# Latent attention's first weights made behind the experts' last units, and one more sequence of the feed-forward in the drain

## What is computed

```python
x = x + _L0_xattn_ref(_layernorm(x, axis=-1), ctx_512, ctx_512)
x = x + _L0_ffn_ref(_layernorm(x, axis=-1), ...)       # top 2 of 8 experts and 4 pass-through routes
x = x + _L1_xattn_ref(_layernorm(x, axis=-1), ctx_512, ...)
x = x + _L1_ffn_ref(_layernorm(x, axis=-1), ...)       # MX-quantised gate, up, down
```

```python
q_hk = (hidden_q @ Wq.T).reshape(Bv, Sv, H, K)
q_big = jnp.einsum('bshk,hkq->bshq', q_hk, w_kc_q)
q_big = _apply_rope(q_big, sin_q[None, :, None, :], cos_q[None, :, None, :])
kv_r = _apply_rope(kv_c, sin_k[None], cos_k[None])
q_r = jnp.einsum('bshq,hqr->bhsr', q_big, W_qr)
k_r = jnp.einsum('bld,hdr->bhlr', kv_r, W_kr)
attn = jax.nn.softmax(jnp.einsum('bhsr,bhlr->bhsl', q_r, k_r), axis=-1)
ctx_c = jnp.einsum('bhsl,bld->bhsd', attn, kv_r)
ctx_lat = jnp.einsum('bhsd,hkd->bhsk', ctx_c, w_kc_kv)
return ctx_lat.transpose(0, 2, 1, 3).reshape(Bv, Sv, H * K) @ Wo.T
```

## Time and profile before

| | |
|---|---|
| median of 3 runs | 785.99 us |
| lowest, highest | 784.54, 786.02 us |
| the profiled execution | 785.92 us |
| its span, first to last instruction | 783.9 us |
| PE, DVE, ACT, POOL busy | 94%, 75%, 52%, 72% of the span |
| mean granted clock of PE | 0.991 of full speed |

### The profile page before, as it was taken

The page is one execution under the profiler, slowest core; times in us unless marked ns, Lnnn a source line. Parts: engine busy times, 40 slices in busy tenths (PEclk is TensorE's granted clock), DMA queues, the critical chain, the costliest instruction groups (busy, mean ns, idle before and its releaser), DMA issues.

```text
span 783.9 us, 15005 instructions
## 1 busy us (share of the span) xinstructions
PE 733.1 (94%) x4872; PEld 534.6 (68%) x4872; DVE 589.0 (75%) x1077; ACT 405.2 (52%) x1084; POOL 564.7 (72%) x588
## 2 busy tenths in 40 slices
PE   3999999978999999798999999999999999987896
PEld 2655555446888888766787777777777777755554
DVE  5898888948777778776565677676767676768996
ACT  1678878732333233326454454655455544573664
POOL 5667777525777767665757778888788888766895
PEclk9999999979999999999999999999999999999999
DMA  9300000013000001132110000000000000000101
GB/s 252 136 1 0 0 0 1 2 52 127 21 21 21 20 22 59 37 125 102 51 52 1 1 2 1 2 1 1 1 1 2 2 1 2 1 1 2 35 28 48
DMA packets 8764, 24.14 MB, mean 31 GB/s; under 512 B 1711, under 2 KB 5167, under 8 KB 8087
## 3 DMA queue, kind: packets, MB, share of 16 engines
q1 hardware_dynamic: 8154, 23.28, 9.0%
q10 hardware_dynamic: 549, 0.08, 0.1%
HBM read 21.26 MB, written 2.10 MB: 30 GB/s over the span
## 4 chain that ended last, share of the span: by engine, by line
PE 44%; DVE 6%; issue 3%; ACT 3%; POOL 2%; DVEq 0%; POOLq 0%; ACTq 0%
PE ps L1413 17%; PE ps L1462 5%; PE ps L1483 4%; PE ps L1429 4%; PE ps L1447 4%; PE ps L1432 3%; PE ps L1497 3%; PE ps L1324 2%; DVE ps L2172 1%; DVE f_h L2160 1%; ACT p L1573 1%; POOL f_h L2280 1%; ACT f_gated L2124 1%; PE ps L2046 1%; ACT l_y L1563 0%
## 5 line engine op out<-in xcount | busy, mean ns | idle before, releaser
L1758 POOL TENSOR_TENSOR q<-turned 64x512 f32<-64x512 f32 x127 | 166.2, 1309 | 24.2 <-DVE turned L1677 11.4
L1413 PE MATMUL ps<-l_yt,a 128*128 128x512 f32 x576 | 144.1, 400 | 4.0 <-DVE a L1631 2.3
L1413 PEld LDWEIGHTS ps<-l_yt,a 128*128 128x128 f32 x576 | 105.1, 189 | 28.9 <-DVE a L1631 2.9
L1745 POOL TENSOR_TENSOR p<-p,l_inverse 128x512 f32<-128x512 f32 x64 | 66.4, 1040 | 60.1 <-DVE l_inverse L1699 59.2
L1677 DVE TENSOR_TENSOR turned<-ps,rope 128x1024 f32<-128x1024 f32 x64 | 78.0, 1219 | 40.6 <-PE ps L1413 36.3
L881 PE MATMUL ps<-yt_experts,wsplit 128*128 (+1 forms) x384 | 97.3, 403 | 0.1
L468 DVE TENSOR_REDUCE negmax<-ps 128x4 f32<-128x512 f32 x128 | 85.1, 685 | 14.9 <-PE ps L291 13.8
L1573 ACT ACTIVATE p<-ps,l_negmax 128x128 f32<-128x128 f32 x256 | 89.8, 388 | 6.5 <-DVE l_negmax L1668 6.5
L881 PEld LDWEIGHTS ps<-yt_experts,wsplit 128*128 128x128 f32 x384 | 71.6, 193 | 14.5 <-DVE inner L1036 0.3
L384 ACT ACTIVATE pt<-ps 128x512 f32<-128x512 f32 x128 | 69.8, 599 | 5.5 <-PE ps L313 3.7
L1590 ACT ACTIVATE qs<-ps 128x512 f32<-128x512 f32 x32 | 19.1, 597 | 102.6 <-PE ps L1432 102.6
(11 more groups left out here) (231 smaller groups left out, 1563.0 us busy)
## 6 DMA issues: line engine op xcount, KB each, us to landing
wide<-in_wide SPq DMA_DIRECT2D x8, 768.0 KB, 4.3
mx_raw<-in_mx SPq DMA_DIRECT2D x8, 384.0 KB, 3.1
x<-in_x SPq DMA_DIRECT2D x4, 512.0 KB, 8.9
ctx_t<-in_ctx_t SPq DMA_DIRECT2D x1, 2048.0 KB, 7.8
out<-x SPq DMA_DIRECT2D x16, 128.0 KB, 1.7
narrow<-in_narrow SPq DMA_DIRECT2D x8, 192.0 KB, 4.1
ktraw<-in_ctx_rows SPq DMA_DIRECT2D x1, 1248.0 KB
wraw<-in_gate SPq DMA_DIRECT2D x1, 1024.0 KB, 18.7
```

The costliest lines, as they stand in the source:

```text
L1413: out = pe.matmul(tile_bank(n, k), a[i][:, pa, kin, k * 128:(k + 1) * 128], yt[j % 2][:, py, kin, :, :].rearrange("p b s -> p (b s)"), sta ...
L1745: pool.tensor_tensor(p[:, head, :, :], p[:, head, :, :], spread(inverse[:, head, :], 2, S), ALU.mult).then_inc(normed[head], 1)
L1758: t = pool.tensor_tensor(out[rows[(head + half) % 2], head, :], turned[rows[head], half, :], turned[rows[head], 2 + half, :], ALU.add)
```

## The change

It has two parts. The first moves pair 0's weights and group 0's turned rows out of latent's beginning into the experts' functions `last`. Their buffers (a new class `Beginning`) take the place of buffers that are dead by then. On the way the first group's normalisation goes from DVE to ACT, with a shift that POOL computes; DVE's block powers come behind the last inner and h; the last `divide` on POOL comes behind a copy of h; and the first narrow load is issued when the last up products are made. The second part raises `EARLY` to 4 and puts the products, the silu and an inverse scale of sequence 3 by hand into the drain.

The core of the diff:

```diff
@@ routed_experts
+        experts.close()
+        g = Beginning(nc, m, latent)
+        halves_ps, rows_ps = [gate_ps[1], up_ps[1]], [weight_ps, last_weight_ps]
+        context_ps, narrow_ps = gate_ps[1], up_ps[1]
@@ sync
             load_wide(sp, m, d, 0)
+            sp.wait_ge(up_made, UNITS)
+            load_narrow(sp, m, d, 0)
@@ tensor, last
                 down(UNITS - 3)
+                pe.wait_ge(m.wide_loaded[0], 16)
+                pe.wait_ge(gated_made, UNITS)
+                queries_products(pe, m.wide[0], 0, halves_ps[0]).then_inc(g.a_made, 1)
+                pe.wait_ge(inner_made, UNITS)
+                queries_products(pe, m.wide[0], 1, halves_ps[1]).then_inc(g.a_made, 1)
                 turn_tiles(CHUNKS - 2)
                 down(UNITS - 2)
+                for k in range(2):
+                    pe.wait_ge(g.y_made, 2 * k + 2)
+                    pe.wait_ge(h_made, UNITS - 1 + k)
+                    turn_pair(pe, m, g.y, k, rows_ps[k]).then_inc(g.y_turned, 1)
                 down(UNITS - 1)
+                pe.wait_ge(g.a_lo, 1)
+                context_products(pe, m.wide[0], context_ps).then_inc(g.c_made, 1)
+                pe.wait_ge(g.a_lo, 2)
+                pe.wait_ge(m.narrow_loaded[0], 16)
+                narrow_products(pe, m.narrow[0], narrow_ps).then_inc(g.b_made, 1)
                 pe.wait_ge(mx_kept, CHUNKS - 1)
                 turn_tiles(CHUNKS - 1)
@@ scalar, last
                 keep_hidden(UNITS - 1)
+                act.wait_ge(var_made, 4)
+                act.wait_ge(rotated, ROTARY_STEPS * GROUPS)
+                for n in range(4):
+                    act.activation(g.y[:, n, :], m.x[:, n, :], ACT.Identity, bias=g.shift[:, n, :],
+                                   scale=m.rstd[:, n, :]).then_inc(g.y_made, 1)
+                for half in range(2):
+                    act.wait_ge(g.a_made, half + 1)
+                    act.activation(g.a0[:, 0, half, :], halves_ps[half][:, 0:3 * 128], ACT.Copy).then_inc(g.a_hi, 1)
                 keep_tiles(CHUNKS - 2)
+                for k in range(2):
+                    act.wait_ge(g.y_turned, k + 1)
+                    act.activation(g.rows(k, 0), pair_of(rows_ps[k]), ACT.Copy).then_inc(g.y_hi, 1)
+                act.wait_ge(g.c_made, 1)
+                act.activation(g.wc[:, 0, 0, :], context_ps[:, 0:E], ACT.Copy).then_inc(g.c_hi, 1)
+                act.wait_ge(g.b_made, 1)
+                act.activation(g.b[0][:, :, :].rearrange("p k c -> p (k c)"), narrow_ps[:, 0:2 * 128],
+                               ACT.Copy).then_inc(g.b_kept, 1)
                 keep_tiles(CHUNKS - 1)
@@ vector, last
-                block_powers(UNITS, GROUPS - 1, EXPERTS - 2)
...
                 hidden(UNITS + 1, 1, last_weight_ps)
+                block_powers(UNITS, GROUPS - 1, EXPERTS - 2)
+                for half in range(2):
+                    dve.wait_ge(g.a_hi, half + 1)
+                    dve.tensor_tensor(g.a0[:, 1, half, :], halves_ps[half][:, 0:3 * 128], g.a0[:, 0, half, :].bitcast(F32),
+                                      ALU.subtract).then_inc(g.a_lo, 1)
                 shift(UNITS + 1, GROUPS - 1, EXPERTS - 1)
+                for k in range(2):
+                    dve.wait_ge(g.y_hi, k + 1)
+                    dve.tensor_tensor(g.rows(k, 1), pair_of(rows_ps[k]), g.rows(k, 0).bitcast(F32),
+                                      ALU.subtract).then_inc(g.y_lo, 1)
                 dve.wait_ge(down_made, UNITS)
                 add_to_x(GROUPS)
@@ gpsimd, last
                 low_part(UNITS - 3, 1)
+                pool.wait_ge(var_made, 2)
+                pool.wait_ge(up_made, UNITS)
+                pool.tensor_tensor(g.shift[:, 0:4, 0], m.mv[:, 0:4, 0], m.rstd[:, 0:4, 0], ALU.mult).then_inc(var_made, 1)
+                pool.wait_ge(var_made, 3)
+                pool.tensor_scalar(g.shift[:, 0:4, 0], g.shift[:, 0:4, 0], -1.0, None, ALU.mult).then_inc(var_made, 1)
+                low_part(UNITS - 2, 0)
                 divide(CHUNKS - 1, EXPERTS - 2)
-                low_part(UNITS - 2, 0)
                 low_part(UNITS - 1, 1)
@@ latent_attention, sync
-        load_narrow(sp, m, d, 0)
@@ latent_attention, tensor
-        queries_weights(0, 0, m.bank(0))
-        queries_weights(0, 1, m.bank(1))
-        turn(0, 0, w_ps)
-        turn(0, 1, q_ps)
-        context_weights(0, m.bank(2))
-        narrow_weights(0, m.bank(3))
@@ latent_attention, vector
-        normalise_first()
-        split_queries_weights(0, 0, m.bank(0))
-        split_queries_weights(0, 1, m.bank(1))
-        split_rows(0, 0, w_ps)
-        split_rows(0, 1, q_ps)
         split_context_weights(0, m.bank(2))
@@ feed_forward
-    EARLY = 3
+    EARLY = 4
@@ feed_forward, tensor
         products(2, 1)
+        products(3, 0)
         turn_p(END, 0)
...
         context(END)
+        products(3, 1)
         project(END, 0)
@@ feed_forward, scalar
-            if n >= 3 and inside(n - 1, B):
+            if n >= EARLY and inside(n - 1, B):
...
         keep_context(END)
+        silu(3)
+        invert_scale(2, 2)
```

More of the change, by code:

```diff
@@ L1233, in rotate_context, with __init__, rows @@
     step.then_inc(rotated, 1)
+class Beginning:
+    def __init__(self, nc, m, scope):
+        sb = lambda name, shape, dt=F32: scope.enter_context(nc.sbuf_tensor(name, shape, dt))
+        sem = lambda name: scope.enter_context(nc.semaphore(f"l_{name}"))
+        self.y = sb("l_y", [S, 4, E])
+        self.yt1 = sb("l_yt1", [128, 2, HALVES, 4, S], F32R)
+        self.wc = sb("wc", [128, 2, HEADS // 2, E], F32R)
+        self.q0, self.qs = sb("q0", [128, 3, 4 * S]), sb("qs", [2 * CE, 4 * S])
+        self.yt0 = sb("l_yt0", [128, 2, HALVES, 4, S], F32R)
+        self.a0 = sb("a0", [128, 2, HALVES, 3 * 128], F32R)
+        self.b = [sb(f"b{i}", [128, 2, 2 * CE]) for i in range(2)]
+        m.narrow = [sb("narrow0", [2 * CE, 3 * 128])]
+        self.shift = sb("l_shift", [S, B, 1])
+        (self.a_made, self.a_hi, self.a_lo, self.b_made, self.b_kept, self.c_made, self.c_hi, self.c_lo, self.y_made,
+         self.y_turned, self.y_hi, self.y_lo) = (
+            sem(n) for n in ("a_made", "a_hi", "a_lo", "b_made", "b_kept", "c_made", "c_hi", "c_lo", "y_made", "y_turned",
+                             "y_hi", "y_lo"))
+    def rows(self, k, part):
+        return self.yt0[:, part, :, 2 * k:2 * k + 2, :]
@@ new lines, in pair_of, with queries_products @@
+def pair_of(ps):
+    return ps.rearrange("p (h b s) -> p h b s", h=HALVES, b=2)
+def queries_products(pe, wide, half, ps):
+    for head in range(2):
+        wq = wide[:, head, half * 128:(half + 1) * 128]
+        most = ps[:, 0:256].rearrange("p (t h c) -> p t h c", t=2, h=2)[:, :, head, :]
+        rest = ps[:, 256:384].rearrange("p (t h c) -> p t h c", t=2, h=2)[:, :, head, :]
+        for out, columns in ((most, wide[:, head, E:E + 128]), (rest, wide[:, head, E + 128:E + CQ])):
+            t = pe.matmul(out, wq, columns.rearrange("p (t c) -> p t c", t=2), start=True, stop=True)
+    return t
@@ new lines, in context_products, with narrow_products, turn_pair @@
+def context_products(pe, wide, ps):
+    for head in range(2):
+        t = pe.matmul(ps[head * CE:(head + 1) * CE, 0:E], wide[:, head, E + CQ:E + CQ + CE],
+                      wide[:, head, E + CQ + CE:], start=True, stop=True)
+    return t
+def narrow_products(pe, narrow, ps):
+    for k in range(2):
+        t = pe.matmul(ps[:, k * 2 * CE:(k + 1) * 2 * CE], narrow[:, k * 128:(k + 1) * 128],
+                      narrow[:, 2 * 128:], start=True, stop=True)
+    return t
+def turn_pair(pe, m, y, k, ps):
+    out = pair_of(ps)
+    for half in range(HALVES):
+        for s in range(2):
+            t = pe.transpose(out[:, half, s, :], y[:, 2 * k + s, half * 128:(half + 1) * 128], m.ident[:, :])
+    return t
@@ L1259, in latent_attention @@
     m.wide.append(sb("wide1", [KDIM, 2, E + CQ + CE + E]))
-    m.narrow = [sb(f"narrow{i}", [2 * CE, 3 * 128]) for i in range(2)]
-    b = [sb(f"b{i}", [128, 2, 2 * CE]) for i in range(PAIRS)]
-    wc = sb("wc", [128, 2, PAIRS, E], F32R)
-    y, shift = sb("l_y", [S, 4, E]), sb("l_shift", [S, B, 1])
-    yt = [sb(f"l_yt{i}", [128, 2, HALVES, 4, S], F32R) for i in range(2)]
+    m.narrow.append(sb("narrow1", [2 * CE, 3 * 128]))
+    b = g.b + [sb(f"b{i}", [128, 2, 2 * CE]) for i in range(2, PAIRS)]
+    wc, y, shift, yt, qs = g.wc, g.y, g.shift, [g.yt0, g.yt1], g.qs
     turned = sb("turned", [128, 2 * TILES, N])
-    q = [sb(f"q{i}", [128, TILES, N]) for i in range(2)]
-    qs = sb("qs", [2 * CE, N])
+    q = [g.q0, sb("q1", [128, TILES, N])]
     negmax, total, inverse = (sb(f"l_{n}", [S, 2, 4]) for n in ("negmax", "total", "inverse"))
@@ L1272, in latent_attention @@
     with ExitStack() as pairs:
-        a = [pairs.enter_context(nc.sbuf_tensor(f"a{i}", [128, 2, HALVES, TILES * 128], F32R)) for i in range(PAIRS)]
+        a = [g.a0] + [pairs.enter_context(nc.sbuf_tensor(f"a{i}", [128, 2, HALVES, TILES * 128], F32R))
```

(1 more changed line is left out.)

62 lines of the change are left out of this document (15 added, 47 removed).

## The result

| | us, median (lowest to highest) | runs |
|---|---|---|
| before | 786.0 (784.5 to 787.6) | 6 |
| the change | 781.6 (780.2 to 783.7) | 6 |
| ratio | 0.9942, 95% interval 0.9922 to 0.9963 | |

A forecast was written before the change was run, and what follows sets the result against it. TensorE was taken to bound the kernel, busy 733.1 of 783.9 us. Front +0.6, clock there +0.1 and drain -3.2 made -2.5, from 785.9 to 783.4 us; range 782.6 to 785.6.

The forecast's parts named there:

- The front, +0.6: End of experts and latent's preparation: pair 1's products wait for their wide load, starting at 338.0 instead of 337.41.
- DVE's new chain: Front: DVE waits for ACT's first copy of a; its sum into x ends at 333.35 instead of 329.68.
- first tile: Front: the first tile starts with the new block at 333.7, 0.8 us earlier than 334.52.
- The missing DMA wait: Sign: PE waits 1.0 to 1.6 us before pair 1's products; if missing, front term wrong and kernel a microsecond faster.
- rival D: Front: PE's clock falls; 3.5 us of it mostly covered by the load wait, 10 us gives 787.0; chance 0.08.
- my +0.1: Front: cost allowed for a short low-clock stretch, mostly covered by PE's 1.3 us wait for the load.
- The drain, -3.2: Drain: fourth sequence's early products and silu let DVE, POOL and the end come 3.2 us earlier (2.1 + 1.1).
- The gated product: Drain: DVE's fourth gated product comes at 712.75 instead of 714.87, 2.1 us earlier.
- The second part, 1.1 from the chain of ACT and POOL: Drain, 720 to 772.6: DVE's idle of 0.4 for ACT and 0.7 for POOL goes, 1.1 us gained.
- another time than before: Sign: the prediction is wrong if the latent steps between front and drain change their time; no term for them.
- Rival B: Drain gains 2.1 only: PE's clock falls again and ACT's chain stays bound to PE; 784.5 us, chance 0.17.
- C: Front: pair 1's wide load shares engines with the narrow and pair 2's loads, 2.4 us later; 785.8, chance 0.10.

The follow-up runs named there:

- again: The changed kernel run once more, unaltered; 782.48 us, ratio to before 0.9958.
- y_later: The changed kernel with ACT's copies of the pair's two halves kept ahead of the four normalisations of y; 780.32 us, ratio to before 0.9926.
- y_wide_bound: The changed kernel with ACT's two halves ahead of y's normalisations, pair 1's wide load early, second sequence's clip bound read from PSUM; 778.74 us, ratio to before 0.9899.
- before_again: The kernel before, unaltered, for another profile; 786.97 us in one run.
- front_alone: The changed kernel with the drain as it was before, so the front's part only; 785.90 us, ratio to before 1.0006.
- drain_new_places: The kernel before with the drain's part, and latent's first tensors at the change's addresses, instruction order kept; 780.95 us, ratio to before 0.9942.
- drain_alone: The kernel before with the drain's part of the change only; 782.31 us, ratio to before 0.9956.

## Why the prediction was wrong

Two of its steps failed. It priced the latent steps between front and drain at nothing, and they took 0.75 us less. And it worked out the drain's gain as 3.2 us from one execution of the old drain: the stages give 2.9 against that execution and 4.1 against another, the medians 3.6. By its own steps:

- **The front, +0.6 (forecast), +0.5 to +0.6 (change, again): right in size, half wrong in mechanism.** DVE's new chain, the block's end and the first tile (1.0 earlier, 0.8 forecast) came as worked out. The missing DMA wait, which I had named as the sign that this term is wrong, did not make the kernel faster: rival D's mild case came true, half clock for 3.1 us, and it covered the load almost exactly. I had priced that overlap as my +0.1 and thought the clock unlikely to matter; y_later shows the wait of 1.28 us that the half clock hid.
- **The drain, -3.2 (forecast), -2.9 by the profile.** The gated product comes 1.6 us earlier and not 2.1, counted from the last query products. The clip that collided with POOL is the difference: it runs 0.5 us longer than before (1.94 and 1.40), and y_wide_bound gave 0.77 back. The second part, 1.1 from the chain of ACT and POOL, came in full: POOL's run starts 2.7 us earlier, 1.6 and 1.1.
- **The same step against the typical execution: -3.6, not -3.2.** Here lies part of the miss. I took the old drain from one profiled execution, with one half-clock stretch. Two other executions of the old order, of before_again and front_alone, show two, and 1.2 us more. I noted that the clock fell after PE's wait of 2.8 us, and did not ask what the wait of 2.25 at 711.2 would do in another execution.
- **Latent's steps, "another time than before" as a sign of error: it was one.** -0.75 us, priced at nothing. The instructions between are the same; their tensors are not in the same places, since the change allocates them in the experts' dead memory. drain_new_places shows that the places alone do it: 352.90 us with them and 353.66 without, all instructions in the old order.
- **The sum.** +0.5 - 0.75 - 2.9 to -4.1 is -3.2 to -4.4, and the two measurements are -4.4 and -3.4. The direction and the two main terms held; the range of 782.6 to 785.6 was too narrow on the fast side, because neither the places nor the other case of the old drain was in it. The failed steps are these two. What the first measurement had beyond 3.4, 1.0 us, is within the two intervals. The mean clocks of its six runs were 0.993 to 0.996, those of again 0.991 to 0.996, so less time at half clock elsewhere may be part of it; that is not shown.
- Rival B (-2.1 alone), C (a slower load: 4.5 us from issue to use, inside the 4.1 to 4.6 of the earlier trace rows) and E (the late p eats the lead) are out by drain_alone, y_later and the drain's stage. front_alone measured 785.9 where its stages, +0.3 and -0.8, make 0.5 us less than before; its runs had mean clocks of 0.989 to 0.991, before's 0.989 to 0.996. Why it lost that half microsecond is open.

## What to carry to other kernels

Look at what an engine waits for together with what its waiting sets off: in three places here TensorE stood for 2.2 to 3 us (at the front with 0.3 us of work between) and then ran some 3 us at half clock; in one of the three it did so in two executions of the old order and not in a third. Where that could be compared it cost another 1.2 to 1.5. At the front a load and such a stretch hid each other, so that removing one showed the other. One profile of a kernel with such waits is one draw: take a second before pricing a term against it. Where a small constant is the second operand of a DVE instruction that runs beside GpSimd, try it in PSUM: here one such clip was worth 0.8 us.
